# A small iota ahead of every scatter and gather that GpSimd issues, in a two-layer graph network kernel

## What is computed

```python
def _graph_conv(x, src, dst, out_norm, in_norm, W, b):
    h = x * out_norm[:, None]
    agg = jax.ops.segment_sum(h[src], dst, num_segments=N_NODES)
    return (agg * in_norm[:, None]) @ W + b
# layer 0: three of them, each followed by elu;  x = layernorm(x + layer 0)
# layer 1:
ea = edge_attr @ W_edge.T + b_edge
msg = relu(x[src] + ea)
h = x + jax.ops.segment_sum(msg, dst, num_segments=x.shape[0])
h = h @ W1.T + b1
h = relu(gamma * (h - mean(h)) * rsqrt(var(h) + 1e-5) + beta)
x = layernorm(x + h @ W2.T + b2)
```

## Time and profile before

| | |
|---|---|
| median of 3 runs | 5930.82 us (5928.49 to 5935.44) |
| span of the profiled execution | 7586.7 us |
| difference | 1655.9 us |
| PE, DVE, ACT, POOL busy | 73%, 56%, 30%, 50% of the span |
| granted clock of PE, mean | 0.862 |

### The profile page before, as it was taken

One profiled execution on the slowest core, in us unless ns is written; L12 is line 12 of the kernel. 1 busy time (PEld: TensorE's weight loads), 2 busy tenths in 40 slices (PEclk: granted clock), 3 DMA queues, 4 the chain that ended last, 5 costly groups with the idle time before them and its releaser, 6 DMA issues.

```text
span 7586.7 us, 112214 instructions
## 1 busy us (share of the span) xinstructions
PE 5556.9 (73%) x39907; PEld 3224.8 (43%) x39908; DVE 4274.3 (56%) x14548; ACT 2271.1 (30%) x4057; POOL 3774.9 (50%) x3824
## 2 busy tenths in 40 slices
PE   6599799997777777778777774666766666665666
PEld 5366566665433333333433332333433333333334
DVE  5488888899533333333444112666666665555556
ACT  2487688873100000000001111333333322222223
POOL 4323233354354544545554556565655666665663
PEclk9799899999888988888888886888888888878887
DMA  2333333331555655556556661111111111111111
GB/s 99 140 130 119 120 142 137 118 118 64 177 173 188 197 177 180 186 186 195 184 185 193 218 207 41 32 34 33 33 33 33 34 33 32 33 33 32 32 32 34
DMA packets 438341, 828.25 MB, mean 109 GB/s; under 512 B 161611, under 2 KB 266983, under 8 KB 430951
## 3 DMA queue, kind: packets, MB, share of 16 engines
q1 hardware_dynamic: 305430, 713.88, 27.9%
q0 software_dynamic: 117952, 81.54, 5.1%
q10 hardware_dynamic: 14400, 25.61, 1.2%
HBM read 621.34 MB, written 199.35 MB: 108 GB/s over the span
## 4 chain that ended last, share of the span: by engine, by line
PE 24%; another core or an unknown queue 14%; issue 13%; DVE 11%; PEld 2%; ACT 1%; PEldq 0%; DVEq 0%; ACTq 0%
PE banks L2182 10%; PE banks L2344 4%; DVE tmp L1673 4%; PE banks L2271 2%; PE banks L2304 2%; PEld banks L2182 2%; DVE onehot L1660 2%; DVE rows_f L1652 2%; PE banks L2324 2%; PE banks L2331 1%; PE banks L2164 1%; DVE rows_f L1680 1%; DVE rows_f L1665 1%; PE banks L2157 1%
## 5 line engine op out<-in xcount | busy, mean ns | idle before, releaser
L1086 POOL DMA_INDIRECT rows_f<-table,src_key x1725 | 1708.4, 990 | 1103.4 <-DVE rows_f L1652 604.3
L1051 POOL DMA_INDIRECT sorted_recs<-onehot,rows x1280 | 1235.5, 965 | 1260.6 <-DMA onehot<-edge_recs_dram 718.7
L2182 PE MATMUL banks<-wide,rows_f 128*128 128x512 fp8e4 (+1 forms) x4900 | 1268.1, 400 | 355.4 <-issue 352.3
L1867 ACT ACTIVATE wide<-banks 128x784 fp8e4<-128x784 f32 x1563 | 1205.6, 825 | 484.6 <-PE banks L2104 340.6
L1006 POOL DMA_INDIRECT onehot<-edge_runs_dram,rows_f x472 | 596.2, 1263 | 1149.1 <-DVE onehot L1196 935.9
L2104 PE MATMUL banks<-rows_f 128*128 128x196 f16 (+2 forms) x7525 | 1004.1, 258 | 223.6 <-ACT wide L1867 138.7
L2104 PEld LDWEIGHTS banks<-rows_f 128*128 128x128 f16 x7525 | 708.5, 152 | 612.1 <-ACT wide L1867 401.9
L2271 PE MATMUL banks<-w_edge_blk,rows 80*128 80x320 f32 x690 | 337.4, 578 | 762.9 <-DVE rows_f L1652 521.6
L1444 DVE SCALAR_TENSOR_TENSOR onehot<-banks,onehot 128x98 f16<-128x98 f32 (+2 forms) x1113 | 295.6, 266 | 989.9 <-PE banks L2164 504.1
L1342 DVE TENSOR_TENSOR rows_f<-hid 128x1024 f16<-128x1024 f16 (+1 forms) x1016 | 679.4, 669 | 300.8 <-PE banks L2104 169.5
L1645 DVE TENSOR_SCALAR rows_f<-banks,iota_p 128x512 f16<-128x512 f32 x294 | 220.7, 751 | 1067.0 <-remote 638.8
(11 more groups left out here) (345 smaller groups left out, 7312.1 us busy)
## 6 DMA issues: line engine op xcount, KB each, us to landing
wide<-counts SPq DMA_DIRECT2D x504, 896.0 KB
counts<-wide SPq DMA_DIRECT2D x50, 3136.0 KB
rows_f<-table,src_key POOLq DMA_INDIRECT x1725
sorted_recs<-onehot,rows POOLq DMA_INDIRECT x1280
sorted_recs<-rows SPq DMA_DIRECT2D x28, 640.0 KB
rows<-attr_dram SPq DMA_DIRECT2D x345, 40.0 KB
onehot<-edge_recs_dram SPq DMA_DIRECT2D x143, 90.0 KB
agg_a<-attr_dram ACTq DMA_DIRECT2D x50, 250.0 KB
```

Source lines behind the costliest of these rows:

```text
L1051: G.indirect_dma_start(out=sorted_recs[:, :], out_offset=bass.IndirectOffsetOnAxis(ap=keys_of(t, t + 1).bitcast(I32), axis=0), in_=taken[g ...
L1086: G.indirect_dma_start(out=g_rows[:, n % ROW_RING, k, :], out_offset=None, in_=table32[:, :], in_offset=bass.IndirectOffsetOnAxis(ap=src_k ...
L1867: A.activation(win_counts[o.half % 2][:, :, d0:d0 + o.quads * QUAD].rearrange("p b (q c) -> p b q c", c=QUAD), counted, ACT.Copy, scale=UN ...
L2182: last = M(acc_d[m % 2].rearrange("p (h d) -> p h d", h=2)[:, 0:h, :], layer_rows[n][:, block, :], pieces[:, PLACE[k], 0:h, c * HALF:(c + ...
```

## The change

One tile of 64 float32 columns (`pause`) is added, and GpSimd writes it with an iota ahead of each indirect DMA of `put_records` and of `gather_units`. Nobody reads it. From the second on, an iota waits for the iota before it (`s_pause`, another name for a semaphore that is free by then). Where a unit has a wait of its own, the iota stands behind that wait.

```diff
+PAUSE = 64
...
+        pause = sb("pause", [P, PAUSE])
...
+        s_pause, PAUSE0 = s_tile, len(SETS)
...
+            paused = [0]
+
+            def pause_once():
+
+                if paused[0]:
+                    pool.wait_ge(s_pause, PAUSE0 + paused[0])
+                G.iota(pause[:, :], [[1, PAUSE]], base=0, channel_multiplier=0, **exact).then_inc(s_pause, 1)
+                paused[0] += 1
+
             def put_records():
...
                         for k in range(UNIT):
                             t = (g * 2 + n) * UNIT + k
+                            pause_once()
                             G.indirect_dma_start(out=sorted_recs[:, :], out_offset=bass.IndirectOffsetOnAxis(ap=keys_of(t, t + 1).bitcast(I32), axis=0),
...
                     for k in range(UNIT):
                         t = (FIRST_UNIT + n) * UNIT + k
+                        pause_once()
                         G.indirect_dma_start(out=g_rows[:, n % ROW_RING, k, :], out_offset=None, in_=table32[:, :],
```

## The result

| | kernel before | changed kernel |
|---|---|---|
| median | 5933.05 us (5928.49 to 5935.44, 4 runs) | 6177.61 us (6174.25 to 6181.29, 4 runs) |
| ratio | | 1.0415, 95% interval 1.0403 to 1.0428 |
| span of the profiled execution | 7586.7 us | 6172.4 us |

The changed kernel is slower by 244.6 us. The prediction said 6173 us. Two further comparisons of the same kernels gave 1.0412 (1.0394 to 1.0429) and 1.0409 (1.0392 to 1.0427).

A forecast was written before the change was run, and what follows sets the result against it. It took GpSimd's issuing of indirect DMAs as the bound of both late stages in timed runs: 5931 + 242 (gathers) + 0 (scatters) = 6173 us; forecast range 5990 to 6293 us, chance 0.45, overall range 5850 to 6470.

The forecast's parts named there:

- The bound, by the budget: Dense stage and edge layer: 3814 us left in timed runs, GpSimd's DMAs want 3965, so it does almost nothing but issue.
- One iota, +0.14 us: Between two indirect DMAs: each iota adds 0.14 us of GpSimd's time, with ends of +0.04 and +0.21.
- the low end: Between two DMAs: the iota runs inside the 0.30 us gap, 0.21 + 0.13 in its place, adding 0.04 us.
- The term of the gathers: Edge layer: 5 x 0.14 = 0.70 us added to each of 345 units, 242 us; ends 69 and 362.
- the sign of being right: Between two gathers: an iota stands there and start to start grows from 1.25 to about 1.39 us.
- The scatters, 0 us: Dense stage: 1430 iotas take 200 us of GpSimd's time, costed at 0 because its waiting covers them.
- the cover: Scatters: GpSimd's waiting for records, 718.7 + 56.5 us, hides the iotas; without it the cost is up to 200 us.
- The wait for the iota before, 0 us: Ahead of each iota: the earlier iota ended a whole DMA before, about 1 us, so the wait never holds; 0 us.
- Rival A: Late stages: GpSimd keeps slack in timed runs, PE and DVE set the pace, no cost; 5931 us, chance 0.13.
- Rival B: Late stages: bursts hold back PE's completions, iotas let them through, so faster; 5741 us at half the gain, chance 0.19.
- Rival C: Slower than forecast: no cover at the scatters, 6373 us; with 0.21 us an iota 6594 us; chance 0.16.
- Rival D: Edge layer: DVE's one-hots and the iotas block each other over the shared port, 103 us more, 6276 us; chance 0.07.

The follow-up runs named there:

- the gathers left out: Kernel before with every unit's fifth gather left out from unit 6 on, 339 fewer; 5524.74 us, ratio 0.9318.
- the undisturbed before: The kernel before, unchanged, profiled again with the experiments; 5932.06 us, span of the profiled execution 5930.1 us.

## Why the prediction was right, and where its steps were not

*The bound, by the budget: right.* It said that the waits of the profile are mostly absent in a timed run and that GpSimd is near its limit. The stages that were guessed at 1990 and 127 us are 1817 and 79; the 221 us between fill the budget of 3814 to 4035, and the two late stages take 1849 + 2185 = 4034.

*One iota, +0.14 us: wrong, 0.075 at the gathers.* The failed step is the choice between the ends. I took the spacing of six iotas as if the 0.30 us stayed whole, and put aside the low end since its row stood behind a rest. That row was right: the iota runs in the gap. What its +0.04 us lacked are an idle time of 0.16 in place of 0.13 behind the iota and a gather that gets longer itself (0.944 to 0.958 us): between two gathers 0.366 us stand in place of 0.305, and with the 0.014 that is 0.075, all middle values. From start to start it is 1.324 us, where the prediction had put 1.39 as the sign of being right and 1.29 as that of an iota inside the gap: nearer to the second. The term of the gathers was 242 us and measures 128 in the trace and 129.5 in the runs.

*The scatters, 0 us: wrong, 112 in the trace and 115.9 in the runs.* The failed step is the cover. It came from the rows of the long execution (718.7 + 56.5 us of waiting for records), though the paragraph before had just said that such waits are mostly not in the timed runs, and though its budget counted scatters and gathers alike. The cover that there is: before, the mean distance of two scatters is 1.293 us and the middle one 1.263, which is 0.030 x 1430 = 43 us in all. Of these 30 us are waits and 13 are scatters that last longer than the middle one. After, the distances are 1.371 and 1.361, 14 us in all, with 5 us of waits. The iotas cost 1430 x 0.098 = 140 us, of which some 25 went into waits: that is all the cover there was, in place of 775.

*The sum: right by luck, through two errors that cancel,* -113 and +116 us. 6173 against 6178 says nothing for the terms. The sign rested on the bound, and that held.

*The wait for the iota before, 0 us:* holds; `<-POOL pause L1052` is 52.0 us in all for 1725 gathers, and each such gap is the same 0.16 us as the others. An iota without this wait was not tried, so the 0 rests on these rows.

*Rival A:* falls by the gathers left out. *Rival B:* falls in these runs, PE's L2304 being the only releaser of note before L1645 with or without iotas, 138.7 and 137.9 us; it holds in the other kind of execution, shown for two iotas and not for one. *Rival C:* right on its mechanism, hardly any cover, and at 116 of its 200 us. *Rival D:* L1687 takes 389 ns against 375 in the undisturbed before, and L1674 288 against 290. The 14 ns come from the iotas of the edge layer: 388 ns with those alone, 376 with the scatters' alone. But the 981 one-hots of this kind that an iota overlapped took 391 ns on average and the others 386, and no iota lasted longer than 0.35 us, which doesn't look like one engine holding up the other for a whole instruction. In all it is 2058 x 14 ns = 29 us on DVE, which doesn't set the pace. On GpSimd's side a gather's mean distance is 0.017 us above the middle one both before and after (1.2664 and 1.249; 1.3406 and 1.324), so the collisions, if they are such, have not grown. The Trainium skill (SBUF — State Buffer, on the shared port pair) has the one of the two engines that comes second block until the other's instruction is over. Single gathers of 1.2 to 1.9 us may be that (29 without iotas, 24 with them), no run here separates it, and the iotas added nothing to it that the end shows.

## What to carry to other kernels

Add an issuing engine's gaps to its busy time before you call it free: GpSimd was "63% busy" and full, and an iota between its DMAs costs what it and the 0.16 us behind it exceed the 0.30 us that stand there anyway, and 0.01 to 0.02 us of a longer DMA. When the profiled execution is much longer than the timed runs, settle by a budget which waits can be in the timed ones, and then use it for every term, covers included. Neither variant here beats the kernel before in an ordinary run; what would is fewer indirect DMAs, at 1.19 us each, shown for one gather in five.

## What the runs showed of the hardware that I had not expected

- Between two indirect DMAs of GpSimd stand 0.30 us (0.305 the middle value in every trace without a filler), and a memset of 0.09 us in there costs next to nothing (1.001, 1.0001 to 1.002).
- The same kernel takes about 5930 us in four sets of runs (medians of 5929 to 5936) and 7742 in another, all 19 runs of it within 1%. The difference is in long rows of indirect DMAs, where the others hear of what PE has ended often over 1 us late, and its cost in those stages vanishes when 0.61 us lie between two DMAs. The record names the chips of the four sets of experiments, 6, 12, 8 and 5 in their order: the long set is the only one on chip 12, and no chip was used twice. The chip of the first profiled execution of the kernel before (7587 us) isn't on record. So whether the chip or the occasion makes the difference, no run here shows.
